# A perceiver layer on one core: the residual x enters the attention's output product on TensorE, and ScalarE writes the sums back

## The reference

```python
x = x + xattn(layernorm(x), ctx, ctx, Wq, Wk, Wv, Wp, focus)   # linear attention; last step is y @ Wp.T
x = x + attn(layernorm(x), W_qkv, b_qkv, W_gate, b_gate)       # q * cumsum(k * v) * sigmoid(gate)
x = x + ffn(layernorm(x), gate_w, up_w, down_w, s_in, s_in_down)  # 4-bit fake quantisation, silu(gate) * up
```

## Time and profile before

| what | value |
|---|---|
| median of the runs | 481.09 us (480.31 to 481.64) |
| the profiled execution's own time | 481.73 us |
| its span, first to last instruction | 480.0 us |
| VectorE busy | 448.4 us, 93% of the span |
| TensorE (matmuls) busy | 383.1 us, 80% |
| ScalarE busy | 361.2 us, 75% |
| GpSimd busy | 7.4 us, 2% |
| mean granted TensorE clock | 0.94 of full speed |

### The profile page before, as it was taken

The page is one execution under the profiler, slowest core; times in us unless marked ns, Lnnn a source line. Parts: engine busy times, 40 slices in busy tenths (PEclk is TensorE's granted clock), DMA queues, the critical chain, the costliest instruction groups (busy, mean ns, idle before and its releaser), DMA issues.

```text
span 480.0 us, 5960 instructions
## 1 busy us (share of the span) xinstructions
PE 383.1 (80%) x1877; PEld 302.1 (63%) x1880; DVE 448.4 (93%) x698; ACT 361.2 (75%) x950; POOL 7.4 (2%) x22
## 2 busy tenths in 40 slices
PE   1996748988988988998998897982998799547675
PEld 1874537877877876876776786882885355213343
DVE  6699999999999999999999999999997878999992
ACT  2569987997997987997887897977339568667763
POOL 2001000000000000000000000000000000000000
PEclk9999879999999999999999999996999999858957
DMA  7990000220220220230230140050200000000001
GB/s 231 355 291 0 0 1 1 89 87 1 89 87 2 87 89 1 81 95 1 62 114 1 45 130 1 1 176 1 77 12 0 2 1 0 1 0 1 23 22 44
DMA packets 27070, 27.65 MB, mean 58 GB/s; under 512 B 1184, under 2 KB 26784, under 8 KB 27040
## 3 DMA queue, kind: packets, MB, share of 16 engines
q1 hardware_dynamic: 26736, 27.27, 17.9%
q0 software_dynamic: 160, 0.01, 0.0%
q10 hardware_dynamic: 144, 0.00, 0.0%
HBM read 26.22 MB, written 1.05 MB: 57 GB/s over the span
## 4 chain that ended last, share of the span: by engine, by line
DVE 76%; issue 9%; PE 5%; ACT 5%; DMA 3%; SPq 1%
DVE focus_words L1278 8%; DVE focus_words L1262 8%; DVE sorted L1317 4%; DVE sorted L1318 4%; DVE merge L1330 4%; DVE level L1287 4%; DVE level L1288 4%; DMA ctx_words<-in_L_ffn_up_w_dram 3%; DVE sorted L1191 3%; DVE amax L1160 2%; DVE sorted L1323 2%; DVE sorted L1322 2%; DVE keymax L1320 2%; DVE merge L1328 2%; DVE rank L1341 2%
## 5 line engine op out<-in xcount | busy, mean ns | idle before, releaser
L807 PE MATMUL bank<-WkT,rows_T 128*128 128x256 f32 x512 | 125.4, 392 | 33.8 <-ACT rows_T L425 33.8
L807 PEld LDWEIGHTS bank<-WkT,rows_T 128*128 128x128 f32 x512 | 95.5, 194 | 51.0 <-ACT rows_T L425 39.5
L902 PE MATMUL bank<-ctx_words,focus_words 128*128 128x257 f32 x512 | 115.0, 382 | 3.5 <-ACT focus_words L524 3.5
L902 PEld LDWEIGHTS bank<-ctx_words,focus_words 128*128 128x128 f32 x512 | 99.3, 197 | 16.0 <-ACT focus_words L524 5.5
L512 ACT ACTIVATE focus_words<-focus_words,shift,ff 128x256 f32<-128x256 f32 x136 | 79.9, 591 | 0.6
L478 ACT ACTIVATE focus_words<-bank 128x256 f32<-128x256 f32 x136 | 50.2, 382 | 26.1 <-PE bank L807 26.1
L524 ACT ACTIVATE focus_words<-focus_words,row_scale 128x256 f32<-128x256 f32 x136 | 56.3, 514 | 12.4 <-DVE row_scale L1280 12.4
L425 ACT ACTIVATE rows_T<-bank 128x512 f32<-128x512 f32 x78 | 44.2, 595 | 17.9 <-PE bank L780 17.9
L780 PE MATMUL bank<-ident,ctx_words 128*128 128x128 f32 x256 | 37.5, 275 | 3.5 <-DMA ctx_words<-in_ctx_dram 2.8
L1361 DVE TENSOR_TENSOR mask<-focus_words,fifth 128x2048 bf16<-128x2048 f32 x17 | 39.0, 2292 | 0.5
L1278 DVE TENSOR_TENSOR focus_words<-focus_words,mask 128x2048 f32<-128x2048 f32 x17 | 38.6, 2271 | 0.0
(11 more groups left out here) (198 smaller groups left out, 582.4 us busy)
## 6 DMA issues: line engine op xcount, KB each, us to landing
ctx_words<-in_ctx_dram SPq DMA_DIRECT2D x32, 512.0 KB, 3.9
ctx_words<-in_L_ffn_gate_w_dram SPq DMA_DIRECT2D x2, 1024.0 KB, 8.2
ctx_words<-in_L_ffn_up_w_dram SPq DMA_DIRECT2D x2, 1024.0 KB, 9.2
xs<-in_x_dram SPq DMA_DIRECT2D x4, 256.0 KB, 4.6
ctx_words<-in_L_ffn_down_w_dram SPq DMA_DIRECT2D x2, 512.0 KB, 10.2
ctx_words<-in_L_ffn_down_w_dram SPq DMA_DIRECT2D x1, 1024.0 KB, 4.9
out_dram<-xs SPq DMA_DIRECT2D x3, 256.0 KB, 2.1
gateT<-in_L_attn_W_qkv_dram SPq DMA_DIRECT2D x1, 512.0 KB, 6.6
```

Of the source, the lines that this page charges most:

```text
L807: ins = pe.matmul(proj_bank[m][:, t * D:(t + 1) * D], rows_T[:, m % 2, 2 * t + k, :], WT[:, k, :], start=(k == 0), stop=(k == KT - 1))
L902: ins = pe.matmul(sum_bank[k][:, 0:GW], heads_half(expo[slot][:, t, :], k), ctx_ring[:, s, t, :], start=(s == 0 and t == 0), stop=(s == PE ...
```

## The change

TensorE's project_out(m) starts each of its two sums with a matmul of the identity by the tile of xs; the first of them stands ahead of the wait for the transposed rows. The products by Wp are accumulated on top. A new ScalarE function, attention_rows(m), copies the bank (128 x 512) into xs. It is called for pairs 0 and 1 behind "mixed2" and ahead of rstd_guess(1), for pair 2 behind "xhat1" and ahead of half_step(0), for pair 3 behind spread_weight(2) and ahead of rstd_guess(2). VectorE's add_attention and add_batch are gone, and attention_stats stands in the same four places. The semaphore attn_added becomes attn_copied, which ScalarE raises; normalise(k) and add_running(t) wait for it too.

```diff
--- before.py
+++ after.py
@@ -256,7 +256,7 @@
         mixed_in_psum = sem("mixed_in_psum")
         mixed_ready = sem("mixed_ready")
         attn_in_psum = sem("attn_in_psum")
-        attn_added = sem("attn_added")
+        attn_copied = sem("attn_copied")
         qkvg_in_psum = sem("qkvg_in_psum")
         gate_k_ready = sem("gate_k_ready")
         gate_read = sem("gate_read")
@@ -460,6 +460,7 @@
             def normalise(k, dst, cols=D):
 
                 act.wait_ge(norm_ready, k)
+                act.wait_ge(attn_copied, 2 * k)
                 for t in range(T)[NORM_TILES[k]]:
                     act.activation(dst[:, t, 0:cols], xs[:, t, 0:cols], ACT.Identity, scale=rstd[:, t:t + 1],
                                    bias=shift_ln[:, t:t + 1]).then_inc(x_hat_ready, 1)
@@ -685,6 +686,12 @@
                 act.activation(xs[:, t, :], bank[4 + (t + 1) % 2][:, (t % 2) * D:(t % 2 + 1) * D], ACT.Copy,
                                scale=out_scale[:, 2:3]).then_inc(rows_out_ready, 1)
 
+            def attention_rows(m):
+
+                act.wait_ge(attn_in_psum, m + 1)
+                act.activation(xs[:, 2 * m:2 * m + 2, :], attn_bank[m][:, :].rearrange("p (t c) -> p t c", t=2), ACT.Copy)\
+                    .then_inc(attn_copied, 1)
+
             def rows_oct(o):
 
                 act.wait_ge(oct_in_psum, FFN_OCTS + o + 1)
@@ -695,12 +702,15 @@
             tail_rows_to_sbuf("mixed0", (kv_in_psum, 2))
             tail_rows_to_sbuf("mixed1", (kv_in_psum, 3))
             tail_rows_to_sbuf("mixed2", (attn_in_psum, 1))
+            attention_rows(0)
+            attention_rows(1)
             rstd_guess(1)
             normalise(1, x_hat2, D - 1)
             save_sums(BATCH)
             tail_rows_to_sbuf("sums3", None)
             tail_rows_to_sbuf("xhat0", (attn_in_psum, 2))
             tail_rows_to_sbuf("xhat1", (attn_in_psum, 3))
+            attention_rows(2)
             half_step(0, slice(0, T * D))
             spread_weight(0)
             act.preload_act_table_set(SIGMOID)
@@ -711,6 +721,7 @@
             act.preload_act_table_set(NAT_LOG_EXP)
             tail_rows_to_sbuf("mixed3", None)
             spread_weight(2)
+            attention_rows(3)
             rstd_guess(2)
             act.preload_act_table_set(SIGMOID)
             gate_tile(2)
@@ -871,7 +882,7 @@
                 if m == 2:
                     pe.wait_ge(mixed_ready, 2)
                 if m == 3:
-                    pe.wait_ge(attn_added, 3)
+                    pe.wait_ge(attn_copied, 3)
                 for t in (2 * m, 2 * m + 1):
                     for k in range(KT):
                         ins = pe.matmul(mix_bank[m][t % 2][:, k * KVW:(k + 1) * KVW], qT[:, t, k, :], kv[:, m, k, :],
@@ -884,11 +895,14 @@
 
             def project_out(m):
 
-                pe.wait_ge(quad_in_sbuf, tail_quad(f"mixed{m}") + 1)
                 for t in range(2):
+                    dst = attn_bank[m][:, t * D:(t + 1) * D]
+                    pe.matmul(dst, ident[:, :], xs[:, 2 * m + t, :], start=True, stop=False)
+                    if t == 0:
+                        pe.wait_ge(quad_in_sbuf, tail_quad(f"mixed{m}") + 1)
                     for k in range(KT):
-                        ins = pe.matmul(attn_bank[m][:, t * D:(t + 1) * D], TAIL_ROWS[f"mixed{m}"][:, 2 * t + k, :],
-                                        WpT[:, k, :], start=(k == 0), stop=(k == KT - 1))
+                        ins = pe.matmul(dst, TAIL_ROWS[f"mixed{m}"][:, 2 * t + k, :],
+                                        WpT[:, k, :], start=False, stop=(k == KT - 1))
                 ins.then_inc(attn_in_psum, 1)
 
             def sum_group(n):
@@ -968,7 +982,7 @@
 
                 pe.wait_ge(kv_prod_ready, t + 1)
                 if t == 1:
-                    pe.wait_ge(attn_added, PAIRS)
+                    pe.wait_ge(attn_copied, PAIRS)
                 if t >= 2:
                     pe.wait_ge(running_added, t - 1)
                 dst = oct_bank[t % 2][:, 0:D]
@@ -1441,19 +1455,14 @@
             def finish_weight(w):
                 times_fp8(w, ffn_fp4[w], ffn_w_ready)
 
-            def add_attention(m):
-                dve.wait_ge(attn_in_psum, m + 1)
-                dve.tensor_tensor(xs[:, 2 * m:2 * m + 2, :], xs[:, 2 * m:2 * m + 2, :],
-                                  attn_bank[m][:, :].rearrange("p (t c) -> p t c", t=2), ALU.add)\
-                    .then_inc(attn_added, 1)
-
             def attention_stats(m):
-                dve.wait_ge(attn_added, m + 1)
+                dve.wait_ge(attn_copied, m + 1)
                 row_stats((2 * m, 2 * m + 1))
 
             def add_running(t):
                 dve.wait_ge(running_in_psum, t + 1)
                 dve.wait_ge(gate_read, t + 1)
+                dve.wait_ge(attn_copied, t // 2 + 1)
                 then(dve.tensor_tensor(gated_sum[:, t % 2, :], oct_bank[t % 2][:, 0:D], q_gated[:, t, :], ALU.mult))
                 dve.tensor_tensor(xs[:, t, :], xs[:, t, :], gated_sum[:, t % 2, :], ALU.add).then_inc(running_added, 1)
 
@@ -1476,10 +1485,6 @@
                 add_running(t)
                 dve.wait_ge(running_added, t + 1)
                 row_stats((t,))
-
-            def add_batch(m):
-                add_attention(m)
-                attention_stats(m)
 
             each = lambda a: a[:, :].rearrange("p (w o) -> p w o", o=1).broadcast_to([P, 3, P])
             flat_w = lambda a: a[:, :, :].rearrange("p w b -> p (w b)")
@@ -1547,14 +1552,14 @@
             mix(1)
             weight_scales()
             mix(2)
-            add_batch(0)
-            add_batch(1)
+            attention_stats(0)
+            attention_stats(1)
             mean_variance(1)
             refine_for_act(1)
             weight_reciprocals()
             dve.wait_ge(ffn_loaded, 48)
             scale_weight(0)
-            add_batch(2)
+            attention_stats(2)
             key_values(3)
             weight_codes(0)
             scale_weight(1)
@@ -1564,7 +1569,7 @@
             weight_codes(1)
             run(0)
             scale_weight(2)
-            add_batch(3)
+            attention_stats(3)
             mean_variance(2)
             refine_for_act(2)
             gate_tile(2)
```

## The result

The changed kernel took 483.59 us in the median of its first four runs (482.74 to 484.27), against 481.08 (480.31 to 481.64) for the kernel before. The ratio is 1.0058 (95% interval 1.0041 to 1.0075). Measured again later, with eight runs against 27 of before, it was 483.07 against 480.66, ratio 1.0048 (1.0031 to 1.0066). I had forecast 481.3 and a range of 480.0 to 483.2. The first of these medians lies above the range, the second inside it, near its upper end.

The account below looks back on a forecast made before the run. The prediction took the bound to be a chain of waits through TensorE and ScalarE, not VectorE, busy 93%. Its terms, + 0.43 + 0.50 - 0.71 = + 0.22 us on 481.09, gave 481.3, range 480.0 to 483.2.

Parts of the forecast that it names:

- the price of the seeds: TensorE's identity matmuls (seeds), which put x into the bank before the products: one adds 0.216 us, a pair 0.43.
- My upper bound: For an identity matmul on TensorE: 0.45 us per matmul, which such a shape takes at half clock.
- Pairs 0 and 1: About 346 to 358 us: TensorE's extra 0.65 us hides in waits, VectorE's aggregation is 0.57 late, nothing reaches the chain.
- Pair 2: 358 to 372 us: identity matmuls push the chain 0.43 us, ScalarE's copy ahead of half_step(0) another 0.50; 0.93 late.
- Pair 3: 372 to 381 us: VectorE's addition goes, saving 0.71 us; ScalarE's copy has 1.7 us of cover.
- Waits: Added waits on attn_copied in normalise and add_running cost nothing, upper end 0.4 us; third copy done two microseconds before mix(3).
- The sum: Up to the aggregation of pairs 2 and 3: + 0.43 + 0.50 - 0.71 = + 0.22 us, making 481.09 into 481.3.
- Rival A: VectorE bounds the stretch, so four additions of 0.68 us come off and nothing is added: 478.4 us; faster, 8%.
- Rival B: TensorE's pauses ahead of 379.62 and 384.14 join into 2.6 us, the clock falls, costing 1.7: 483.0 us; 24%.
- rival C: ScalarE's copy of pair 3 ends 1.7 us later, VectorE waits, the 0.71 is not saved: 482.0 us; 3%.

Follow-up runs that it names:

- pair 3 alone: Against the kernel before, only pair 3 changed, pairs 0 to 2 added on VectorE: ratio 0.9995; with running(1) also waiting for stats_ready 3: 0.9993 and 0.9995.

## Why the prediction was wrong

**The step that failed** is the price of the seeds: "eight of those take 1.89 us with a last one of 0.38, so one adds 0.216, a pair of them 0.43". 0.216 us per matmul instruction is right. But a matmul call on f32 tiles is two instructions in these traces (a transpose of f32, L780, and a matmul of bf16, L1023, are one): the eight of a project_out are four calls (two tiles by two halves of the rows), and two seeds are four instructions, 0.86 us. The row said x8 and the source two loops of two; I did not hold them side by side, and so the section on the kernel speaks of eight matmuls. The second source, the x2 of L1043, I read as two matmuls as well; it is one call. My upper bound, half clock at 0.45 per seed, has by chance the right size, but I kept it out of the sum.

- **Pairs 0 and 1.** "So 0.65 less 0.63 remains: nothing" fails with it. Three seeds out of their cover are 1.30 us; 1.30 - 0.63 is 0.67, measured 0.60 at the last sum_group. ScalarE's and VectorE's slack did hold: the late aggregation (12.14 in place of 11.02) reaches nothing.
- **Pair 2.** 0.43 for the seeds was 0.86; 0.50 for the copy was 0.48. The order of the argument was right: TensorE has nothing to hide in, and the copy stands ahead of half_step(0).
- **Pair 3.** - 0.71 was measured as - 0.71 or - 0.72 in every variant that has the change there. The cover was 1.2 us and not 1.7, for the same reason.
- **Waits.** Nothing was seen of their cost. Without the seeds all of them stay, and the aggregation comes 0.23 us earlier, which is 0.48 less 0.71. The third copy was done 3.1 us before TensorE's mix(3), not two.
- **The sum.** 0.60 + 0.86 + 0.48 - 0.71 = 1.23 in place of 0.22.
- **Rival A** (VectorE's time is the time) falls: 2.7 us less of its work, and in no variant is the middle shorter by more than the 0.7 of pair 3.
- **Rival B** (the clock falls) came true beside the forecast and not in place of it. Its pause was forecast as 2.6 and is 2.20, since pair 3's seeds, too, take 0.43 more and end TensorE's work ahead of the pause later. Its price was forecast as 1.7 and is 1.65 in the one trace that has it. Two of the first four times, four of the next eight and one of the last three are in the upper group; if all 7 of 15 are such falls, they add about 0.8 us to the mean. 1.23 + 0.8 makes 2.0, against 2.5 and 2.4 between the medians and 2.5 and 2.1 between the means. Had the seeds been priced rightly, I would have forecast 482.3, inside the range, with a chance for B to go over it.
- **The prediction's rival C** (the copy of pair 3 late) did not happen.

The Trainium skill ("TensorE: Matmul & The Clock Gate", section "HAM oscillation — how this bites in real kernels") says that waits between bursts of matmuls put the clock back to half. One trace here agrees. The others go further: the same pause of 2.20 us in the same program was followed by half clock in one of five traced executions, so the program alone does not decide it. What does was not found.

What stays open: how many of the upper times are such falls, the last 0.1 to 0.5 us of the difference, which the intervals don't resolve, and whether pair 3 alone is faster at the end. On the second: over five traces against four, the fixed point comes 0.3 us later in the mean and the part behind the middle is 0.2 longer, both within their spread. On the third: the middle is shorter by 0.72 to 0.73 us in each of three traces; the three ratios (0.9995, 0.9993, 0.9995) lie on the fast side of 1 without excluding it. Taken together as independent measurements they make about 0.9994, give or take 0.0009 (an estimate), which puts the full saving, 0.9985, at the very edge. It may be that only part of it reaches the end; nothing here shows why.

## What to carry to other kernels

Before pricing an added matmul, divide the count of a trace row by the calls in the source: here an f32 matmul call was two instructions. An addition moved from the busiest engine to two others gains only where that engine's wait ends last; of the four pairs, changed alike, one gained 0.71 us and one lost 1.34. And when a wait is removed from TensorE, look at what pause its neighbours now form: a longer one can cost the clock, in some executions only, and a wait put back can be worth more than the time that it holds (without seeds, in one trace each, the middle was 1.38 us shorter with the added wait).

## What was not expected of the hardware

The same kernel, with the same pause of 2.20 us, was granted full clock behind it in four traced executions and half in a fifth, worth 1.65 us of 482. Its fifteen executions fell in two groups, 481.9 to 483.0 and 483.6 to 484.3; the fifth is in the upper one, the four in the lower. The kernel before, too, has a spread of 3 us in the part behind 411 us (65.6 to 68.6) with a middle that repeats to 0.02 us; between its longest and its shortest it is mainly the granted clock of the last matmuls that differs (0.50 or 1.00 from 470.7 to 477.1). What a change costs up to 411 us can thus be told by such fixed points to hundredths of a microsecond, where the times of the whole kernel did not tell 0.7 us from nothing.
